# Layer 1 attention: GpSimd's additions of probabilities, each split into two of 512 columns

## The chip, the core and the metric

The kernel runs on one core of a Trainium2 chip. The core has five engines that each work through a program of their own and wait for one another by semaphores: TensorE (PE in the profile, its weight loads PEld), VectorE (DVE), ScalarE (ACT), GpSimd (POOL) and SyncE (SP), which issues the DMAs here. The metric is the device time of one execution in microseconds, from three runs before the change.

## What is computed

Two layers, each an attention and a feed-forward part whose results are multiplied and added to the input x of 4 x 1024 tokens by 512 values. Only layer 1's attention matters here, softmax attention with 16 heads of 32 values:

```python
def proj(w):
    return (x @ w.T).reshape(b, t, NH, HD).transpose(0, 2, 1, 3)
q, k, v = (proj(wq), proj(wk), proj(wv))
q, k = apply_rope(q, k, sin, cos)
att = jnp.einsum('bhqd,bhkd->bhqk', q, k) * (1.0 / math.sqrt(HD))
att = jax.nn.softmax(att, axis=-1)
y = jnp.einsum('bhqk,bhkd->bhqd', att, v)
```

The sum of the exponentials over all keys, by which softmax divides, is what the additions of this change build up.

## The kernel before

Four stages follow one another: layer 0 attention, layer 0 feed-forward, layer 1 attention, layer 1 feed-forward. `layer1_attention` works on 16 groups (4 batches by 4 groups of 4 heads). Its ticks are written out for the first four and the last ones; between them a hardware loop (`Fori` in `ticks`) runs them, two ticks to a pass of its body.

A tick has 32 units. In a unit ScalarE computes the probabilities of one pair of heads for 128 keys and 512 queries: two activations (L1170) read the scores from `ps_sc0` and `ps_sc1` and write the two halves of one of eight tiles `probs` (128x2x512). Units 0 to 15 are for the first 512 queries and 16 to 31 for the rest; inside each, a unit is a block of keys and a pair of heads.

For each unit whose block of keys isn't the first, `add` on GpSimd (L1102) adds the unit's `probs` tile to `summed`, all 1024 columns in one instruction. That is 28 additions a group. In the last group every other one is VectorE's: 434 on GpSimd in all and 14 on VectorE. An addition waits until both activations of its unit are done (`exp_done`) and until the addition two units before is. ScalarE waits, before it writes a tile, for the addition eight units back, since that one reads the same tile (`RING = 8`). At the end of each half TensorE sums `summed` over its partitions (den, L1343), ScalarE copies that (L1145), VectorE inverts it in four pieces (L1253), and GpSimd multiplies the output by it (`y_out`, L1210, 128x512).

In the same tick the next group is prepared, one chunk of 128 tokens in every two units of the first 16, chunks 0 to 7: TensorE projects (L61), ScalarE copies to `qk` and `v` (L1185, L1186), VectorE turns q and k by the rope tables (L1237, L1238, L1239, then L1242), ScalarE casts (L1156, L1158), VectorE subtracts what the cast has kept (L1245 for `q_tok`, L1246 for `k_tok`), TensorE transposes q and k (L1355) into `ps_prep`, and ScalarE copies them to `q_st` and `k_st` (L1198). The six VectorE instructions read both operands from SBUF, as GpSimd's do. Between them VectorE reduces the scores of a first pass from PSUM to their maxima (L1259, one input). TensorE's order in a tick is fixed by `prepare`, `scores`, `pv` and `maximum`; q transposes of a chunk wait for `stacked` (both `q_tok` and `k_tok`) and for the bank `ps_prep` to be read.

Of the kernel before, what the change touches and what calls it, by code (L numbers as in the profile page):

```python
# [7 lines left out]
ALU = mybir.AluOpType  # L8
# [18 lines left out]
def need(eng, sem, count):  # L27

    if isinstance(count, int) and count <= 0:
        return  # L30
    eng.wait_ge(sem, count)  # L31


def live(c, n):

    return not isinstance(c, int) or 0 <= c < n
# [867 lines left out]
def layer1_attention(nc, xt_in, wqkvT, rope_cos, rope_sin, yt_out):  # L904
# [13 lines left out]
    RING = 8  # L918
# [3 lines left out]
    with ExitStack() as ctx:  # L922
# [60 lines left out]
        probs = [sb(f"probs{i}", [P, 2, DIM]) for i in range(RING)]  # L983
# [98 lines left out]
        def adds_with(g, u):  # L1082


            if u < 0:
                g, u = g - 1, u + UNITS
            qb, kt, pair = u // LAST, max(u // 2 % CPB, 1), u % 2
            if isinstance(g, int) and g == NT - 1:
                n = (CPB - 1) * qb + kt
                return (dve_added, n) if pair else (added, ADDS * QB * g + n)  # L1090
            return added, ADDS * (QB * g + qb) + 2 * (kt - 1) + pair + 1

        def add(eng, m, u):

            g, kt, total = m - 1, u // 2 % CPB, summed[u // LAST][u % 2]
            need(eng, exp_done, 2 * (UNITS * g + u + 1))
            if kt > 1:
                need(eng, *adds_with(g, u - 2))
            elif live(g - 1, NT):
                need(eng, prep_done, prep_use(*((m, ("den", 1)) if u >= LAST else (m - 1, ("den", 0))))[1] + 1)  # L1100
            old = probs[(u - 2) % RING] if kt == 1 else total
            eng.tensor_tensor(total[:, :, :], old[:, :, :], probs[u % RING][:, :, :], ALU.add).then_inc(adds_with(g, u)[0], 1)  # L1102

        S = 4
        sched = (0, 4, NT, NT)
# [98 lines left out]
        @block.gpsimd  # L1204
        def _(pool):
            def scale_out(g, qb):
                need(pool, y_copied, QB * g + qb + 1)
                need(pool, y_stored[qb], 16 * g)
                need(pool, inverted, PIECES * (QB * g + qb + 1))
                pool.tensor_tensor(y_out[qb][:, :], y_sb[qb][:, :], inv_den[:, :], ALU.mult).then_inc(y_ready, 1)  # L1210

            def tick(m, p):

                for u in range(UNITS):
                    last = isinstance(m, int) and m == NT
                    if u // 2 % CPB and live(m - 1, NT) and not (last and u % 2):
                        add(pool, m, u)
                    for qb in range(QB):
                        if u == INVERT_AT[qb] + PIECES and live(m - 1 - qb, NT):
                            scale_out(m - 1 - qb, qb)  # L1220
            ticks(pool, *sched, tick)
            scale_out(NT - 1, 1)

        @block.vector
        def _(dve):
# [48 lines left out]
            def tick(m, p):  # L1274
                for u in range(UNITS):
                    if isinstance(m, int) and m == NT and u % 2 == 0 and u and (u - 1) // 2 % CPB:
                        add(dve, m, u - 1)
                    todo = [e[1] for e in maxes(u) if exists(m, e)]

                    for c in range(CPB):  # L1280
                        if u == PREP_STEP * c // 2 + 1 and live(m, NT):
                            for step in range(2):
                                chunk(m, p, c, step)
                                if todo:
                                    maximum(m, todo.pop(0))
                    for a in todo:
                        maximum(m, a)
                    for c in range(CPB):
                        if u == PREP_STEP * c // 2 + 2 and live(m, NT):
                            chunk(m, p, c, 2)  # L1290
                    for qb in range(QB):
                        if 0 <= u - INVERT_AT[qb] < PIECES and live(m - 1 - qb, NT):
                            invert(m - 1 - qb, qb, u - INVERT_AT[qb])
            ticks(dve, *sched, tick)
            add(dve, NT, UNITS - 1)
            for step in range(PIECES):
                invert(NT - 1, 1, step)
# [364 lines left out]
```

## Time and profile before

| | us |
|---|---|
| runs before, median of 3 | 3529.43 |
| lowest and highest run | 3527.44, 3536.01 |
| profiled execution | 3538.25 |
| its span (first to last instruction) | 3536.5 |

The profile is of one execution. Busy shares tell how much an engine works, not who is waited for; that is read from the waits and from the timeline. In the timeline a row is a run of like instructions: start, length, engine, line, operation, what it writes and reads, how many, and in brackets the idle time of its engine before it with what ended that. On VectorE and GpSimd an instruction's length includes what it waits for inside, after its semaphores are satisfied.

### The profile page before, as it was taken

The page shows a single profiled execution, that of the slowest core. Times are in us where ns is not written, and L with a number is a line of the kernel's source. Part 1 is how long each engine was busy: PE and PEld are TensorE (multiplying, and loading weights), DVE is VectorE, ACT ScalarE, POOL GpSimd, SP SyncE. Part 2 cuts the span into 40 slices and gives each one's busy share as a digit, 9 for nine tenths or more (in the row PEclk, how much of TensorE's full clock was granted, in tenths as well). Part 3 has the DMA queues.
Part 4 walks back from the last instruction along what each step waited for, and adds up shares of the span by engine and source line. Part 5 has one row for each costly group of instructions (what it writes and reads, how often), then busy time and mean ns, then how long its engine had stood idle before and what let it go on. Part 6 is the DMA issues. An engine that isn't in the chain of part 4 may idle for free. (4 is left out here: it accounts for less than half of the span.)

```text
span 3536.5 us, 53506 instructions
## 1 busy us (share of the span) xinstructions
PE 3178.8 (90%) x16548; PEld 2231.9 (63%) x16548; DVE 2400.1 (68%) x3422; ACT 1662.3 (47%) x3006; POOL 1501.5 (42%) x1085
## 2 busy tenths in 40 slices
PE   5999999919999996999999989999999939999999
PEld 4766666617888885655555555555555418888887
DVE  4455555478888884788888888888888844444444
ACT  2211121106777774566666666666666622222222
POOL 1000000033333331377777777777777732112111
PEclk9999999959999998899999999999999969999999
DMA  2000000031222223111111111111111032122121
GB/s 83 25 24 24 30 24 24 18 113 66 90 89 89 89 78 127 60 51 54 54 55 55 54 55 50 54 54 49 54 55 54 20 150 75 60 74 68 65 74 48
DMA packets 97104, 215.26 MB, mean 61 GB/s; under 512 B 11408, under 2 KB 27792, under 8 KB 96400
## 3 DMA queue, kind: packets, MB, share of 16 engines
q1 hardware_dynamic: 95472, 210.14, 17.6%
q10 hardware_dynamic: 1440, 2.76, 0.2%
q8 instruction: 95, 1.56, 0.2%
q14 instruction: 97, 0.79, 0.1%
HBM read 162.54 MB, written 50.33 MB: 60 GB/s over the span
## 5 line engine op out<-in xcount | busy, mean ns | idle before, releaser
L1102 POOL TENSOR_TENSOR l_attn_summed<-l_attn_summed,l_attn_probs 128x1024 f32<-128x1024 f32 x372 | 884.8, 2402 | 161.0 <-ACT l_attn_probs L1170 160.7
L1259 DVE TENSOR_REDUCE l_attn_maxima<-l_attn_ps_max 128x2 f32<-128x1024 f32 x512 | 608.9, 1210 | 127.9 <-PE l_attn_ps_max L1367 125.3
L1170 ACT ACTIVATE l_attn_probs<-l_attn_ps_sc 128x512 f32<-128x512 f32 x1024 | 578.7, 601 | 217.7 <-PE l_attn_ps_sc L1323 200.2
L1323 PE MATMUL l_attn_ps_sc<-l_attn_q_st,l_attn_k_st 128*128 128x512 f32 x1024 | 451.9, 454 | 15.4 <-ACT l_attn_probs L1170 12.6
L70 PE MATMUL l_ffn_ps_gu<-l_ffn_w_gu,l_ffn_xt 128*128 128x512 f32 (+1 forms) x1536 | 345.6, 378 | 47.0 <-DMA l_ffn_xt<-xt_chunks 47.0
L1367 PE MATMUL l_attn_ps_max<-l_attn_k_st,l_attn_q_st 96*128 96x512 f32 x1024 | 352.9, 428 | 28.4 <-DVE l_attn_maxima L1259 28.3
L1510 POOL TENSOR_TENSOR l_ffn_mixed<-l_ffn_gate,l_ffn_up 128x512 f32<-128x512 f32 (+1 forms) x96 | 115.2, 1199 | 522.6 <-DVE l_ffn_up L1559 519.0
L70 PEld LDWEIGHTS l_ffn_ps_gu<-l_ffn_w_gu,l_ffn_xt 128*128 128x128 f32 x1536 | 279.7, 189 | 87.6 <-DMA l_ffn_xt<-xt_chunks 48.7
L1323 PEld LDWEIGHTS l_attn_ps_sc<-l_attn_q_st,l_attn_k_st 128*128 128x128 f32 x1024 | 193.9, 194 | 222.0 <-ACT l_attn_probs L1170 139.1
L1308 PE MATMUL l_attn_ps_y<-l_attn_probs,l_attn_v 128*32 128x512 f32 x2048 | 286.1, 632 | 16.5 <-issue 12.3
L61 PE MATMUL l_attn_ps_prep<-l_attn_wqkv_hi,l_attn_xt 128*128 (+1 forms) x1016 | 271.2, 348 | 31.8 <-DMA l_attn_xt<-xt_chunks 30.9
L1367 PEld LDWEIGHTS l_attn_ps_max<-l_attn_k_st,l_attn_q_st 96*128 96x128 f32 x1024 | 193.6, 200 | 120.1 <-DVE l_attn_maxima L1259 76.1
L1102 POOL TENSOR_TENSOR l_attn_summed<-l_attn_probs 128x1024 f32<-128x1024 f32 x62 | 147.6, 2388 | 253.9 <-ACT l_attn_probs L1170 253.8
L281 POOL TENSOR_TENSOR l_attn_rstd<-l_attn_mean_var,l_attn_ln_eps 128x1 f32<-128x1 f32 x32 | 6.1, 190 | 551.0 <-DVE l_attn_mean_var L356 551.0
L70 PE MATMUL l_ffn_ps_fc<-l_ffn_t_fc,l_ffn_ct_hi 128*128 128x512 f32 x512 | 214.8, 420 | 12.8 <-issue 6.6
L61 PEld LDWEIGHTS l_attn_ps_prep<-l_attn_wqkv_hi,l_attn_xt 128*128 128x128 f32 x1016 | 181.3, 191 | 62.2 <-DMA l_attn_xt<-xt_chunks 22.6
L319 ACT ACTIVATE l_attn_ot_hi<-l_attn_ps_o 128x512 fp32r<-128x512 f32 x32 | 19.1, 598 | 400.2 <-PE l_attn_ps_o L494 400.2
L70 PE MATMUL l_ffn_ps_out<-l_ffn_t_proj,l_ffn_ht_hi 128*128 128x512 f32 x512 | 205.4, 401 | 0.0
L70 PE MATMUL l_ffn_ps_fc<-l_ffn_t_fc,l_ffn_ct_lo 128*128 128x512 f32 x512 | 204.6, 400 | 0.0
L70 PE MATMUL l_ffn_ps_out<-l_ffn_t_proj,l_ffn_ht_lo 128*128 128x512 f32 x512 | 202.8, 396 | 0.0
L61 PE MATMUL l_attn_ps_prep<-l_attn_wqkv_lo,l_attn_xt 128*128 (+1 forms) x508 | 173.0, 341 | 0.0
L1245 DVE TENSOR_TENSOR l_attn_q_tok<-l_attn_qk,l_attn_q_tok 128x128 fp32r<-128x128 f32 x128 | 117.8, 921 | 76.0 <-ACT l_attn_k_tok L1158 75.8
(232 smaller groups left out, 6584.7 us busy)
## 6 DMA issues: line engine op xcount, KB each, us to landing
l_attn_xt<-xt_chunks SPq DMA_DIRECT2D x128, 512.0 KB, 3.3
xt_chunks<-l_ffn_xt SPq DMA_DIRECT2D x32, 512.0 KB, 2.8
l_ffn_xt<-xt_chunks SPq DMA_DIRECT2D x32, 512.0 KB, 3.4
l_attn_xin<-in_x SPq DMA_DIRECT2D x32, 256.0 KB, 2.7
s<-l_attn_s_sb SPq DMA_DIRECT2D x32, 256.0 KB, 2.0
l_ffn_xa<-in_x SPq DMA_DIRECT2D x32, 256.0 KB, 2.6
l_ffn_xb<-in_x SPq DMA_DIRECT2D x32, 256.0 KB, 2.9
l_ffn_s_sb<-s SPq DMA_DIRECT2D x32, 256.0 KB, 3.6
```

Source lines behind the costliest of these rows:

```text
L61: mm = pe.matmul(out, a(k), w(k), start=(n == 0), stop=(n == 3 * slices - 1))
L70: mm = pe.matmul(out, a(k), w(k), start=(first and k == ks[0] and n == 0), stop=(last and k == ks[-1] and n == 1))
L281: pool.tensor_tensor(rstd[b][:, :], mean_var[b][:, 1:2], bn_eps[:, :], ALU.add).then_inc(rstd_ready, 1)
L319: act.activation(ot_hi[b][:, :, :], ps_o[:, :, :], ACT.Copy).then_inc(ot_hi_ready, 1)
L1102: eng.tensor_tensor(total[:, :, :], old[:, :, :], probs[u % RING][:, :, :], ALU.add).then_inc(adds_with(g, u)[0], 1)
L1170: act.activation(probs[u % RING][:, i, :], ps_sc[i][:, :, :].rearrange("p a n -> p (a n)"), ACT.Exp, scale=ATT_SCALE).then_inc(exp_done, 1)
L1245: dve.tensor_tensor(qs[:, :, 2 * HD:3 * HD], x[:, 0, :, :], fp32(qs[:, :, 0:HD]), ALU.subtract).then_inc(stacked, 1)
L1259: dve.tensor_reduce(maxima[:, j, h:h + 2, half:half + 1], ps_max[bank][:, :, :], AX.X, ALU.max).then_inc(max_read[bank], 1)
L1308: mm = pe.matmul(ps_y[HD * h:HD * h + HD, :], v[p][:, kt, HD * h:HD * h + HD], probs[(2 * j + h // 2) % RING][:, h % 2, :], start=(kt == 0 ...
L1323: pe.matmul(ps_sc[i][:, :, :].rearrange("p a n -> p (a n)"), k_st[p][:, h, P * kt:P * kt + P], q_st[p][:, h, DIM * qb:DIM * qb + DIM], sta ...
L1367: mm = pe.matmul(dst[:, i, :], q_st[b][0:AUG, h + i, P * j:P * j + P], k_st[b][0:AUG, h + i, DIM * half:DIM * half + DIM], start=True, sto ...
L1510: pool.tensor_tensor(mixed[p][:, lo:hi], gate[p][:, lo:hi], up[p][:, lo:hi], ALU.mult).then_inc(mixed_ready, 1)
```

## The change

`add` issues two instructions, one for each head of the pair (`i` is 0 or 1), each of 128x512. Only the second one counts up the semaphore. The waits ahead of the first are as before, and so is the place of every addition in its engine's order. `add` is also what VectorE runs in the last group, so its 14 additions are split in the same way.

```diff
             old = probs[(u - 2) % RING] if kt == 1 else total
-            eng.tensor_tensor(total[:, :, :], old[:, :, :], probs[u % RING][:, :, :], ALU.add).then_inc(adds_with(g, u)[0], 1)
+            for i in range(2):
+                ins = eng.tensor_tensor(total[:, i, :], old[:, i, :], probs[u % RING][:, i, :], ALU.add)
+            ins.then_inc(adds_with(g, u)[0], 1)
```

## Rows read from the trace of the kernel before

**Rows 1.** The page, section 1: busy us of each engine.

```profile
PE 3178.8 (90%) x16548; PEld 2231.9 (63%) x16548; DVE 2400.1 (68%) x3422; ACT 1662.3 (47%) x3006; POOL 1501.5 (42%) x1085
```

**Rows 2.** Busy time by stretch: stretch, length, then busy us of each engine.

```profile
core 0: us, PE busy (x) PEld busy (x) DVE busy (x) ACT busy (x) POOL busy (x), PEclk, DMA share, GB/s
1451.00:2804.00 1353.00, 1231.12 (x6584) 730.85 (x6584) 1117.05 (x1347) 875.56 (x1857) 1020.65 (x446) 0.97 0.16 52
```

**Rows 3.** Waits of PE, 1451 to 2864: total us, times, longest us.

```profile
PE l_attn_ps_max L1367 <- DVE l_attn_maxima L1259: 25.6, 45, 1.2
PE l_attn_ps_sc L1323 <- ACT l_attn_probs L1170: 12.6, 41, 0.9
...
PE l_attn_ps_prep L1355 <- DVE l_attn_k_tok L1246: 10.5, 34, 0.7
```

**Rows 4.** The page, section 5: busy us, mean ns, then idle before, and its releaser.

```profile
L1102 POOL TENSOR_TENSOR l_attn_summed<-l_attn_summed,l_attn_probs 128x1024 f32<-128x1024 f32 x372 | 884.8, 2402 | 161.0 <-ACT l_attn_probs L1170 160.7
...
L1102 POOL TENSOR_TENSOR l_attn_summed<-l_attn_probs 128x1024 f32<-128x1024 f32 x62 | 147.6, 2388 | 253.9 <-ACT l_attn_probs L1170 253.8
```

**Rows 5.** Groups of instructions of DVE in the stage, same columns.

```profile
L1242 DVE TENSOR_TENSOR l_attn_qk<-l_attn_turned_part,l_attn_swapped 128x128 f32<-128x128 f32 x128 | 154.3, 1205 | 1.8
...
L1245 DVE TENSOR_TENSOR l_attn_q_tok<-l_attn_qk,l_attn_q_tok 128x128 fp32r<-128x128 f32 x128 | 117.8, 921 | 76.0 <-ACT l_attn_k_tok L1158 75.8
L1246 DVE TENSOR_TENSOR l_attn_k_tok<-l_attn_qk,l_attn_k_tok 128x128 fp32r<-128x128 f32 x128 | 101.5, 793 | 0.0
```

**Rows 6.** Timeline of DVE in chunk 0 of one group.

```profile
1815.92 1.38 DVE L1237 TENSOR_TENSOR l_attn_turned_part<-l_attn_qk,l_attn_cos_t 128x128 f32<-128x128 f32 x1 [2.80 <-ACT l_attn_qk L1185]
...
1817.37 0.21 DVE L1239 TENSOR_TENSOR l_attn_swapped<-l_attn_qk,l_attn_sin_t 128x64 f32<-128x64 f32 x1
...
1818.63 0.28 DVE L1242 TENSOR_TENSOR l_attn_qk<-l_attn_turned_part,l_attn_swapped 128x128 f32<-128x128 f32 x1
...
1819.97 1.33 DVE L1245 TENSOR_TENSOR l_attn_q_tok<-l_attn_qk,l_attn_q_tok 128x128 fp32r<-128x128 f32 x1
1821.23 0.28 DVE L1246 TENSOR_TENSOR l_attn_k_tok<-l_attn_qk,l_attn_k_tok 128x128 fp32r<-128x128 f32 x1
```

**Rows 7.** Timeline of POOL, DVE, ACT and PE in chunk 5 of the same group.

```profile
1843.01 4.79 POOL L1102 TENSOR_TENSOR l_attn_summed<-l_attn_summed,l_attn_probs 128x1024 f32<-128x1024 f32 x2 [2.18 <-ACT l_attn_probs L1170]
1845.48 2.47 DVE L1246 TENSOR_TENSOR l_attn_k_tok<-l_attn_qk,l_attn_k_tok 128x128 fp32r<-128x128 f32 x1
1847.26 0.60 ACT L1198 ACTIVATE l_attn_k_st<-l_attn_ps_prep 128x512 fp32r<-128x512 f32 x1 [0.83 <-PE l_attn_ps_prep L1355]
1848.00 0.47 PE L1355 MATMUL l_attn_ps_prep<-l_attn_ident_r,l_attn_q_tok 128*96 128x128 f32 x4 [0.24 <-DVE l_attn_k_tok L1246]
```

**Rows 8.** Timeline of POOL through units 18 to 31 and beyond.

```profile
1783.16 4.71 POOL L1102 TENSOR_TENSOR l_attn_summed<-l_attn_probs 128x1024 f32<-128x1024 f32 x2 [7.07 <-ACT l_attn_probs L1170]
1787.84 18.73 POOL L1102 TENSOR_TENSOR l_attn_summed<-l_attn_summed,l_attn_probs 128x1024 f32<-128x1024 f32 x8
1806.53 1.28 POOL L1210 TENSOR_TENSOR l_attn_y_out<-l_attn_y_sb,l_attn_inv_den 128x512 f32<-128x512 f32 x1
1807.77 9.39 POOL L1102 TENSOR_TENSOR l_attn_summed<-l_attn_summed,l_attn_probs 128x1024 f32<-128x1024 f32 x4
1818.67 2.48 POOL L1102 TENSOR_TENSOR l_attn_summed<-l_attn_probs 128x1024 f32<-128x1024 f32 x1 [1.51 <-ACT l_attn_probs L1170]
```

**Rows 9.** Timeline: ACT's activations of unit 31, PE's q transposes of chunk 0.

```profile
1808.34 1.30 ACT L1170 ACTIVATE l_attn_probs<-l_attn_ps_sc 128x512 f32<-128x512 f32 x2 [0.83 <-PE l_attn_ps_sc L1323]
...
1821.89 0.41 PE L1355 MATMUL l_attn_ps_prep<-l_attn_ident_r,l_attn_q_tok 128*96 128x128 f32 x4
```

**Rows 10.** Timeline of POOL and DVE at the same place, behind the loop's branch.

```profile
2078.05 9.31 POOL L1102 TENSOR_TENSOR l_attn_summed<-l_attn_summed,l_attn_probs 128x1024 f32<-128x1024 f32 x4
...
2088.72 0.29 DVE L1237 TENSOR_TENSOR l_attn_turned_part<-l_attn_qk,l_attn_cos_t 128x128 f32<-128x128 f32 x1 [1.94 <-ACT l_attn_qk L1185]
```

**Rows 11.** Timeline of POOL and PE at the stage's end.

```profile
2861.20 6.72 POOL L1102 TENSOR_TENSOR l_attn_summed<-l_attn_summed,l_attn_probs 128x1024 f32<-128x1024 f32 x2
...
2868.01 1.94 PE L1343 MATMUL l_attn_ps_prep<-l_attn_summed,l_attn_ones 128*32 128x512 f32 x8 [2.56 <-POOL l_attn_summed L1102]
```

## Prediction

> **What bounds the kernel now.** I read the busy shares first: TensorE is busy for 90% of the span, VectorE 68%, GpSimd 42% [rows 1]. The change touches one stage alone, layer 1's attention, so the next view is the stage's own stretch. In 1353 us of it (all but its start and its end) TensorE is busy for 1231.12 us, VectorE for 1117.05 and GpSimd for 1020.65 [rows 2]. TensorE leads and its 122 us of gaps are the most that anything in this stage could give back. The table of waits says who ends them [rows 3]: VectorE's maxima 25.6 us, ScalarE's probabilities 12.6 us, VectorE's k_tok 10.5 us. GpSimd is in none of these rows. Its 434 additions of 128x1024 take 884.8 + 147.6 = 1032.4 us, and 161.0 + 253.9 = 414.9 us of idle time stand before them, nearly all of it until ScalarE has written the probabilities [rows 4]. So GpSimd follows; it doesn't lead.
>
> It does act on VectorE. The instructions with two SBUF operands that make q and k (L1242, L1245, L1246) have means of 1205, 921 and 793 ns [rows 5], and the same instructions take 0.28 us when GpSimd is idle [rows 6]. In the three groups that is 154.3 + 117.8 + 101.5 = 373.6 us against 384 x 0.28 = 107.5 us, so about 266 us of VectorE's time is waiting inside its own instructions. The plainest case is a k_tok of 2.47 us [rows 7]: GpSimd's two additions run from 1843.01 to 1847.80, and k_tok starts at 1845.48, one boundary (about 1845.4) after which the second addition had begun, and ends at 1847.95, 0.15 us after it. I read this as: a two-operand VectorE instruction waits until GpSimd's current instruction ends, gets through at that boundary, and the next one waits for the next boundary. Reductions from PSUM (L1259) do not show it.
>
> **Price of a split addition.** Removed: 434 additions on GpSimd and 14 on VectorE (last group) of 1024 columns. Added: twice as many of 512. GpSimd's eight additions in a row take 18.73 us, 2.34 each from start to start, and a 512-column instruction in the same run (y_out) starts at 1806.53 with the next at 1807.77: 1.24 us [rows 8]. Two are 2.48, so a split addition costs 0.14 us more. The low bound is zero (time by columns alone); the high bound, from y_out's own 1.28 us taken twice against 2.34, is 0.22. I take 0.14, because it is start to start on both sides. In all 434 x 0.14 = 61 us more on GpSimd, against 414.9 us of idle time. That would be free if it were spread evenly. [...]
>
> **Where the 61 us aren't free.** In the second part of each group (units 16 to 31) GpSimd has no idle time. From 1783.16 its 14 additions and one y_out run back to back until 1817.16 [rows 8]. With the change this run ends 14 x 0.14 = 2.0 us later, at about 1819.1. Two things could wait for it. The first is ScalarE, which may not write a probability tile before the addition eight units back has read it. The last two activations of the group start at 1808.34 [rows 9] and the last addition ends at 1817.16: 8 us of lag, some 3.5 additions, out of 8. With 2.0 us more it is about 4.5. This wait stays away.
>
> The second is chunk 0 of the next group, where VectorE starts q and k just as this run ends. In the trace L1237 begins at 1815.92, is held until 1817.30, L1238 and L1239 then pass an idle GpSimd, and L1242 starts at 1818.63, 0.04 us ahead of GpSimd's next addition at 1818.67, and takes 0.28 us. L1245 is held until 1821.30, k_tok ends at 1821.51 [rows 6], and TensorE, which starts the q transposes at 1821.89 [rows 9], has some 0.3 us to spare. With the change the boundaries are 1816.64, 1817.88 and 1819.12: L1237, L1238 and L1239 each wait for one, and the chain leaves at about 1819.25 instead of 1817.58. A maximum of 1.15 us follows, so L1242 starts at about 1820.35. GpSimd's next addition, ready since 1818.67, runs 1819.12 to 1821.60 with a boundary at 1820.36. If L1242 catches that boundary k_tok is done at about 1822.0 and TensorE loses 0.1 to 0.4 us. If it misses, it waits until 1821.6, k_tok ends near 1823.3, and TensorE loses about 1.5 us. I take 0.6 us for such a group.
>
> This holds for about half of the groups. The loop's body has two groups, and after its branch all engines start later: there GpSimd's run ends at 2087.36 and L1237 starts only at 2088.72 [rows 10]. A run that ends at 2089.3 then costs L1237 one boundary (0.6 us), after which GpSimd has nothing to do, and k_tok has spare time. So **+8 x 0.6 = +5 us** for chunk 0.
>
> **The other seven chunks.** Here VectorE's waits get shorter, which is what a split can give. For the k_tok of 2.47 us the halves end at about 1844.25, 1845.5, 1846.75 and 1848.0; q_tok goes at 1845.5, k_tok at 1846.75, about 1.1 us earlier. But TensorE's q transposes at 1848.00 also need the bank that ScalarE's k_st copy frees, and this copy ends at 1847.86 [rows 7], 0.14 us ahead; that copy follows TensorE's transposes of the chunk before, whose k_tok was done long ago. What is late next is thus equally late, and almost nothing comes back, although the row is labelled k_tok. Most of the 10.5 us [rows 3] is of this kind: I take **-1 us**. In chunks 1 and 2 L1242 is released earlier and ScalarE's casts with it, so v's copy may be some 0.1 us earlier: two chunks by 15 groups is -3 us. Against that q_tok and k_tok leave when GpSimd's burst of two additions ends, and a burst ends 0.28 us later, some 0.1 us of which may show: +2 us. Together **-1 us**. VectorE's maxima (25.6 us) mostly hold TensorE in the second part, where VectorE has maxima and reciprocals and nothing with two SBUF operands, so they don't move: 0.
>
> **The end of the stage.** TensorE's last den waits for GpSimd's last addition: the two last additions run 6.72 us from 2861.20, and den starts at 2868.01 after 2.56 us of idle time [rows 11]. They alternate with VectorE's additions, split as well. Two splits are 0.28 us, and handing over at twice as many boundaries about as much again: **+0.5 us**.
>
> **Sum.** +5 - 1 - 1 + 0.5 = +3.5 us, from 3538.25 (span 3536.5 and 1.75 us around it) to about 3542. The profiled execution is 8.8 us above the median of the runs, 3529.43; the same difference on the median gives 3533. What a measurement of this kernel can tell from no change is about 0.3%, 10.6 us, so this is a forecast of no difference.
>
> **Rivals.**
> First, faster: VectorE's shorter waits do reach TensorE. For it: 266 us of waiting is much, and k_tok and maxima together end 36.1 us of TensorE's gaps [rows 3]. Halved, with ScalarE's later copies moving up as well: -18 us, 3511. Against it: the tie of k_tok with k_st, and that a chain of two-operand instructions under a busy GpSimd leaves only where the burst ends. It would need TensorE's order to have no other late input. The Trainium skill's "SBUF — State Buffer", section "Who interferes with whom", says that VectorE with two SBUF inputs and a GpSimd instruction that reads SBUF exclude each other for the whole instruction, the second blocking until the first ends. By that rule the longest wait falls from a whole addition to half of one, and it speaks for this rival; the trace agrees with the mechanism, an instruction of 2.47 us beside additions of 2.34 [rows 7, 8].
> Second, slower: the tail of GpSimd's run costs chunk 0 the missed boundary every time, and the groups behind the branch as well. For it: the 0.04 us by which L1242 now gets ahead. Price: 1.5 us by 15 groups is 22 us, 3552. It decides from the point where the run's end passes L1242's lead: 0.04 us of delay on VectorE is enough there, and 14 x 0.14 is far above it. Against it: a missed boundary costs 1.24 us and no longer 2.4, and behind the branch the run ends 1.4 us ahead of chunk 0 [rows 10].
> Third, it doesn't do what it says: GpSimd goes from one half to the other with no wait between them, and VectorE gets no turn there. Then VectorE's waits stay at 2.4 us, only the 61 us are added, and chunk 0 loses by the late run alone: +5 for chunk 0, nothing back, +0.5 at the end, about +6 us, 3535.
>
> **How the numbers follow.** Forecast (3533, within 0.3%) 0.57; faster rival 0.15; slower rival 0.17; no turn between the halves 0.11. The range reaches to the faster rival's milder half and the slower one's: 3516 to 3548. Faster by over 0.3% (below 3518.8): 0.14. Slower by over 0.3% (above 3540.0): 0.20, which is the slower rival and a part of the third. Within: 0.66.
>
> **What would show it.** In the profile after: GpSimd's additions of 512 columns at about 1.3 us each with starts 1.24 us apart; their sum near 1100 us; no long wait of ScalarE on summed; L1242, L1245 and L1246 never over about 1.4 us, with a sum well below 373.6 us (right), or still up to 2.4 us (third rival). In chunk 0, L1237 to L1239 held one after another, and TensorE's wait on k_tok there. If TensorE's wait rows shrink by more than 10 us, the first rival is right. I am wrong as well if a split addition costs much more than 0.14 us: at about 0.5 us each GpSimd's run would reach the ring's eight units.

## The result and the profile after

The changed kernel takes 3565.91 us (median of 4 runs, 3558.22 to 3568.51), the kernel before, run beside it, 3529.24 us (3527.44 to 3536.01). The ratio is 1.0097, with an interval of 1.0076 to 1.0118: the change costs 37 us. The forecast was 3533, and the range ended at 3548. The profiled execution took 3568.51 us, 30.3 us more than that of before, which lay 9.0 us above its median.

The page after, section 1, busy us of each engine [rows 1]:

```profile
PE 3194.1 (90%) x16548; PEld 2242.7 (63%) x16548; DVE 2359.9 (66%) x3436; ACT 1667.5 (47%) x3006; POOL 1568.9 (44%) x1519
```

GpSimd's additions (before: [rows 4]), then VectorE's instructions for q and k (before: [rows 5]). In the kernel after, every line behind the edit has moved down by two:

```profile
L1103 POOL TENSOR_TENSOR l_attn_summed<-l_attn_summed,l_attn_probs 128x512 f32<-128x512 f32 x744 | 943.5, 1303 | 126.7 <-ACT l_attn_probs L1172 126.4
L1103 POOL TENSOR_TENSOR l_attn_summed<-l_attn_probs 128x512 f32<-128x512 f32 x124 | 157.7, 1297 | 246.7 <-ACT l_attn_probs L1172 246.7
```

```profile
L1244 DVE TENSOR_TENSOR l_attn_qk<-l_attn_turned_part,l_attn_swapped 128x128 f32<-128x128 f32 x128 | 65.8, 514 | 1.8
L1247 DVE TENSOR_TENSOR l_attn_q_tok<-l_attn_qk,l_attn_q_tok 128x128 fp32r<-128x128 f32 x128 | 67.4, 527 | 73.9 <-ACT l_attn_k_tok L1160 73.5
L1248 DVE TENSOR_TENSOR l_attn_k_tok<-l_attn_qk,l_attn_k_tok 128x128 fp32r<-128x128 f32 x128 | 133.6, 1044 | 0.0
```

The additions and these three groups of VectorE behave as forecast. The additions are 943.5 + 157.7 = 1101.2 us (forecast: near 1100), and the three groups of VectorE fell from 373.6 to 266.8 us, with none of their instructions over 1.4 us (before, up to 2.5). L1237, L1238 and L1239, which the prediction's sum left out, grew by 48 us together. The loss is TensorE's. Its waits in the stage, 1451 to 2904 (before: [rows 3]): total us, times, longest us:

```profile
PE l_attn_ps_prep L1357 <- ACT l_attn_q_st L1193: 35.8, 15, 2.4
PE l_attn_ps_max L1369 <- DVE l_attn_maxima L1261: 29.4, 47, 3.9
PE l_attn_ps_prep L61 <- DMA l_attn_xt<-xt_chunks: 23.0, 12, 2.6
...
PE l_attn_ps_prep L1357 <- ACT l_attn_k_st L1200: 9.0, 38, 0.2
PE l_attn_ps_prep L1345 <- DVE l_attn_summed L1103: 4.1, 1, 4.1
```

The largest row, for q_st, was 35.8 us before as well. The row that has grown is the one for xt, and the prediction doesn't mention it. The same row of the kernel before, in 1451 to 2864:

```profile
PE l_attn_ps_prep L61 <- DMA l_attn_xt<-xt_chunks: 7.7, 9, 1.1
```

TensorE now waits 15.3 us longer for a load of `xt`, the input of the next group's projections. The stage as a whole, columns as in [rows 2], before and then after (what comes ahead of 1390 is unchanged, and the last stage takes 660.5 us before, 660.8 after):

```profile
1390.00:2876.00 1486.00, 1334.23 (x7040) 784.93 (x7040) 1200.54 (x1459) 938.59 (x1986) 1072.66 (x466) 0.96 0.16 52
```

```profile
1390.00:2906.00 1516.00, 1350.49 (x7040) 797.37 (x7040) 1159.83 (x1474) 945.12 (x1987) 1138.80 (x900) 0.94 0.16 51
```

The stage is 30 us longer. 13.7 us of that are idle time of TensorE (151.8 to 165.5). The other 16.3 us are busy time for the same 7040 matmuls: the mean granted clock fell from 0.96 to 0.94. Counted in the trace's clock record from the first group to the last, TensorE's clock was at 1.2 GHz for 71.7 us before and for 109.2 us after.

Where in the stage: 3.3 us lie ahead of the first group and of the first addition. In the thirteen traces of this study that point lies anywhere from 1449.8 to 1455.9 us, so this is no effect of the change. From there TensorE's entries into each half of a group (its matmuls on `minus_max`) cut the stage into parts. The first parts (units 0 to 15) of 15 groups have grown by 23.3 us, that of the last group by 4.8, and the second parts are 1.8 us shorter in all. Before, a first part takes about 52 us, and about 54 in four of the five groups behind the loop's branch; after, it takes 53 to 56 in all but the first.

**One place.** Where group 4 is followed by group 5, in the kernel before (SPq is SyncE's queue of DMAs; `y_out` is in [rows 8]):

```profile
1808.25 0.40 SPq L1128 DMA_DIRECT2D yt_chunks<-l_attn_y_out  x1
1809.01 0.94 SPq L1115 DMA_DIRECT2D l_attn_xt<-xt_chunks  x2
1813.00 0.61 PE L61 MATMUL l_attn_ps_prep<-l_attn_wqkv_hi,l_attn_xt 128*128 x2 [0.90 <-DMA l_attn_xt<-xt_chunks]
```

and after:

```profile
1814.57 1.30 POOL L1212 TENSOR_TENSOR l_attn_y_out<-l_attn_y_sb,l_attn_inv_den 128x512 f32<-128x512 f32 x1
1816.31 0.40 SPq L1130 DMA_DIRECT2D yt_chunks<-l_attn_y_out  x1
1817.07 0.94 SPq L1117 DMA_DIRECT2D l_attn_xt<-xt_chunks  x2
1821.08 0.61 PE L61 MATMUL l_attn_ps_prep<-l_attn_wqkv_hi,l_attn_xt 128*128 x2 [2.36 <-DMA l_attn_xt<-xt_chunks]
...
1823.33 0.84 PE L61 MATMUL l_attn_ps_prep<-l_attn_wqkv_hi,l_attn_xt 128*128 x2
1825.05 0.83 DVE L1239 TENSOR_TENSOR l_attn_turned_part<-l_attn_qk,l_attn_cos_t 128x128 f32<-128x128 f32 x1 [5.31 <-ACT l_attn_qk L1187]
```

This is a chain of five links. `y_out` of the first 512 queries stands in GpSimd's queue behind ten additions of the second half. SyncE stores it to DRAM, and in SyncE's queue the loads of `xt` for the next group stand behind that store. The first load is issued 0.76 us after the store and TensorE's projections start 4.0 us after the load, before and after alike. Against the end of unit 31's last activation, `y_out` starts 3.1 us ahead in nearly every group before and 1.7 us ahead in nearly every group after: ten splits at 0.14 us are 1.4 us. TensorE's wait grows by the same, from 0.90 to 2.36 us. And behind this longer gap the granted clock falls to 1.2 GHz: a pair of L61 takes 0.84 us instead of 0.52. In the 10 us from the first L61 on the mean granted clock is 1.00 before and 0.83 after. A pair at 0.84 has lost 0.32 us, 38%; of the 37.5 us more at this clock that makes some 14 by estimate, about the 16.3 us of busy time. Before, the clock fell at the start of 4 groups, all behind the loop's branch, now at that of 14. That the longer gap brings the lower clock is argued from this, and it isn't so every time: in the profile of experiment 1's first kernel, gaps of 1.9, 2.5 and 2.2 us before L61 (at 1543, 1816 and 1909 us) had the full clock for 10 us behind them.

VectorE is hardly held at this place. In the whole trace after, ahead of the last group, a single two-operand instruction was passed over at a boundary of GpSimd's (L1239 at 1551.16, 1.63 us).

**The last group**, in which VectorE makes half of the additions (before, the end was [rows 11]):

```profile
2838.53 5.75 DVE L1103 TENSOR_TENSOR l_attn_summed<-l_attn_probs 128x512 f32<-128x512 f32 x2
2839.55 2.52 POOL L1103 TENSOR_TENSOR l_attn_summed<-l_attn_probs 128x512 f32<-128x512 f32 x2
...
2845.47 0.73 PE L1369 MATMUL l_attn_ps_max<-l_attn_k_st,l_attn_q_st 96*128 96x512 f32 x2 [3.93 <-DVE l_attn_maxima L1261]
...
2890.05 9.01 DVE L1103 TENSOR_TENSOR l_attn_summed<-l_attn_summed,l_attn_probs 128x512 f32<-128x512 f32 x6
2891.77 6.74 POOL L1103 TENSOR_TENSOR l_attn_summed<-l_attn_summed,l_attn_probs 128x512 f32<-128x512 f32 x4
2899.20 1.08 PE L1345 MATMUL l_attn_ps_prep<-l_attn_summed,l_attn_ones 128*32 128x512 f32 x4 [4.14 <-DVE l_attn_summed L1103]
```

Two halves on VectorE take 5.75 us beside GpSimd's run, and a maximum that stands behind them comes 3.9 us late. At the very end the six halves of VectorE and the four of GpSimd alternate. Den waits 4.14 us instead of 2.56, and now for VectorE. From the start of the last group to its middle TensorE takes 34.0 us instead of 29.2.

### The profile page after: what moved, and what is told of

It is laid out like the page before. It is cut to its first block and busy times, and to the rows that moved or that the text cites. A ratio compares the mean times of both kernels' runs of the same rounds, so it can differ in the third digit from the quotient of the medians.

```text
span 3566.8 us, 53954 instructions
## 1 busy us (share of the span) xinstructions
PE 3194.1 (90%) x16548; PEld 2242.7 (63%) x16548; DVE 2359.9 (66%) x3436; ACT 1667.5 (47%) x3006; POOL 1568.9 (44%) x1519
## 5 line engine op out<-in xcount | busy, mean ns | idle before, releaser
L1103 POOL TENSOR_TENSOR l_attn_summed<-l_attn_summed,l_attn_probs 128x512 f32<-128x512 f32 x744 | 943.5, 1303 | 126.7 <-ACT l_attn_probs L1172 126.4
L61 PE MATMUL l_attn_ps_prep<-l_attn_wqkv_hi,l_attn_xt 128*128 (+1 forms) x1016 | 280.8, 359 | 48.4 <-DMA l_attn_xt<-xt_chunks 47.2
L1310 PE MATMUL l_attn_ps_y<-l_attn_probs,l_attn_v 128*32 128x512 f32 x2048 | 287.3, 634 | 15.3 <-issue 11.1
L1103 POOL TENSOR_TENSOR l_attn_summed<-l_attn_probs 128x512 f32<-128x512 f32 x124 | 157.7, 1297 | 246.7 <-ACT l_attn_probs L1172 246.7
L61 PEld LDWEIGHTS l_attn_ps_prep<-l_attn_wqkv_hi,l_attn_xt 128*128 128x128 f32 x1016 | 186.8, 197 | 81.5 <-issue 41.8
L61 PE MATMUL l_attn_ps_prep<-l_attn_wqkv_lo,l_attn_xt 128*128 (+1 forms) x508 | 178.5, 351 | 0.0
L61 PE MATMUL l_attn_ps_proj<-l_attn_wqkv_hi,l_attn_xt_hi 128*128 128x512 f32 x384 | 161.1, 420 | 2.3 <-DVE l_attn_xt_lo L360 1.4
```

Of the source, the lines that this page charges most:

```text
L61: mm = pe.matmul(out, a(k), w(k), start=(n == 0), stop=(n == 3 * slices - 1))
L1103: ins = eng.tensor_tensor(total[:, i, :], old[:, i, :], probs[u % RING][:, i, :], ALU.add)
L1310: mm = pe.matmul(ps_y[HD * h:HD * h + HD, :], v[p][:, kt, HD * h:HD * h + HD], probs[(2 * j + h // 2) % RING][:, h % 2, :], start=(kt == 0 ...
```

## Experiments

Each is compared with the kernel before, run beside it on the same chip (its median was 3532.18 us for experiments 1 and 4, 3532.21 us for 2, 3 and 6). Only the timed ratios carry a verdict; the profile of each is one execution.

**1. Which half of the change.** Split only units 16 to 31 (the diff), or only units 0 to 15 (`u < LAST` in its place), in all groups but the last:

```diff
+            if u >= LAST and not (isinstance(m, int) and m == NT):
+                for i in range(2):
+                    ins = eng.tensor_tensor(total[:, i, :], old[:, i, :], probs[u % RING][:, i, :], ALU.add)
+                ins.then_inc(adds_with(g, u)[0], 1)
+            else:
                 eng.tensor_tensor(total[:, :, :], old[:, :, :], probs[u % RING][:, :, :], ALU.add).then_inc(adds_with(g, u)[0], 1)
```

> Only the additions of units 16 to 31 are split, and none in the last group. Theory A: all of the delay of y_out is made here, so the groups are as slow as in the changed kernel (+2 us in most, about +25), without the 5 us of the last group: 3553 to 3561. Theory B: part of it, as chunk 0 also meets a late run, but first-part additions keep 2.4 us waits: 3545 to 3560.

Measured: 3560.47 us, ratio 1.0083 (1.0064 to 1.0103). Waits of TensorE:

```profile
PE l_attn_ps_prep L61 <- DMA l_attn_xt<-xt_chunks: 24.8, 14, 2.5
PE l_attn_ps_prep L1360 <- DVE l_attn_k_tok L1251: 9.9, 34, 0.9
```

> Only the additions of units 0 to 15 are split, and none in the last group. Theory A: GpSimd has idle time there, y_out isn't later, so nothing is lost: 3526 to 3532. Theory B, or any cost of shorter instructions against VectorE (more boundaries, more waits in a chain): slower by 5 us or more, 3535 to 3550.

Measured: 3527.59 us, ratio 0.9986 (0.9976 to 0.9996). Waits of TensorE:

```profile
PE l_attn_ps_prep L61 <- DMA l_attn_xt<-xt_chunks: 7.3, 9, 1.3
PE l_attn_ps_prep L1360 <- DVE l_attn_k_tok L1251: 0.6, 1, 0.6
```

The loss comes from the second half's additions, where VectorE has nothing to gain. In the first half, where its two-operand instructions are, the split is worth 4.6 us (1.4 to 8.5 by the interval), and TensorE's wait for k_tok goes with it.

**2. The last group alone.** Only the last group's additions are split:

```diff
+            if isinstance(m, int) and m == NT:
+                for i in range(2):
```

> Only the last group's 28 additions are split (14 on GpSimd, 14 on VectorE). The trace of the changed kernel had the stage's end 4 to 5 us longer, with one VectorE half-addition of 4.1 us: +4 to +5 us, 3533 to 3537. If that long wait only came from GpSimd's late run ahead of the last group, +1 us or less.

Measured: 3536.11 us, ratio 1.0010 (1.0000 to 1.0019), so +3.9 us. Its first part is 33.3 us instead of 29.2. The three parts of the change add up to 28.3 - 4.6 + 3.9 = 27.6 us, against 36.7 for the whole; the intervals of the whole and of the first term are 7 us wide to each side, so these can't tell whether the remaining 9 us are real.

**3. No split at all, only a later run.** One spare addition of 128x512 on GpSimd in each group but the last, directly ahead of `y_out`, and in another kernel directly behind it. The run is then 1.24 us longer, but VectorE's boundaries are as before:

```diff
+        spare = sb("spare", [P, DIM])
...
+                            if qb == 0 and not last:
+                                pool.tensor_tensor(spare[:, :].rearrange('p (a n) -> p a n', n=P), fp32(w_hi[:, 0, :, 0:P]), fp32(w_hi[:, 1, :, 0:P]), ALU.add)
```

> The kernel before, no addition split, with one spare addition of 512 columns on GpSimd in each group but the last, right ahead of the y_out of the first 512 queries (its result is used by nobody). It makes y_out and the end of GpSimd's run later by some 1.24 us, the split by 1.4 and 2.0 us. Theory C (the harm is the lateness of that run, by whichever end it reaches TensorE: SyncE's queue behind y_out, or VectorE's two-operand instructions in chunk 0): groups lose as in the changed kernel, some +2 us in most, 3545 to 3557. Theory D (the harm is in the shorter additions themselves): at most the 0.9 us waits grow a little, 3530 to 3535.

Measured ahead of `y_out`: 3557.84 us, ratio 1.0074 (1.0057 to 1.0091). Its wait rows and the timeline at one place:

```profile
PE l_attn_ps_max L1370 <- DVE l_attn_maxima L1262: 28.0, 48, 1.9
PE l_attn_ps_prep L61 <- DMA l_attn_xt<-xt_chunks: 21.7, 12, 2.6
...
PE l_attn_ps_prep L1358 <- DVE l_attn_k_tok L1249: 8.2, 31, 0.8
```

```profile
1810.53 1.28 POOL L1222 TENSOR_TENSOR l_attn_spare<-l_attn_wqkv_hi 128x512 f32<-128x512 f32 x1
1811.77 1.30 POOL L1211 TENSOR_TENSOR l_attn_y_out<-l_attn_y_sb,l_attn_inv_den 128x512 f32<-128x512 f32 x1
1813.01 9.34 POOL L1103 TENSOR_TENSOR l_attn_summed<-l_attn_summed,l_attn_probs 128x1024 f32<-128x1024 f32 x4
1813.51 0.40 SPq L1129 DMA_DIRECT2D yt_chunks<-l_attn_y_out  x1
```

> The same spare addition, but right behind that y_out: y_out, its store and the load of chunk 0 are on time, only the run's end is 1.24 us later. Theory A (all by SyncE's queue): 3530 to 3533. Theory C with both ends: VectorE's L1237 in chunk 0 waits until the later end and TensorE waits for k_tok or maxima: 8 groups by 0.6 to 2 us, 3535 to 3548; the share of the queue is then e5 less this one.

Measured behind `y_out`: 3546.08 us, ratio 1.0038 (1.0027 to 1.0049); its ten runs lie between 3535.5 and 3553.8. Its wait rows, and the timeline:

```profile
PE l_attn_ps_max L1370 <- DVE l_attn_maxima L1262: 32.2, 51, 1.9
PE l_attn_ps_prep L1358 <- DVE l_attn_k_tok L1249: 14.1, 40, 0.9
PE l_attn_ps_prep L61 <- DMA l_attn_xt<-xt_chunks: 9.7, 11, 1.6
```

```profile
1817.06 9.40 POOL L1103 TENSOR_TENSOR l_attn_summed<-l_attn_summed,l_attn_probs 128x1024 f32<-128x1024 f32 x4
...
1824.02 2.58 DVE L1240 TENSOR_TENSOR l_attn_turned_part<-l_attn_qk,l_attn_cos_t 128x128 f32<-128x128 f32 x1 [2.82 <-ACT l_attn_qk L1186]
```

A spare addition ahead of `y_out` brings 25.6 us of loss (just above the 3545 to 3557 expected), most of what the split of the second half cost (28.3 us), with the same wait on xt, first parts of about 54 us as well, and 102.4 us at 1.2 GHz. So a later run is enough for most of the loss, without any halves. VectorE has little part in it: the rows for its maxima and k_tok are 28.0 and 8.2 us here, 25.6 and 10.5 in [rows 3], and none of its instructions is passed over at a boundary.

The same 1.24 us behind `y_out` cost 13.9 us, in another way: VectorE reaches chunk 0 while GpSimd still runs. In the row above it starts 0.1 us ahead of a boundary (about 1824.12), isn't let through there, and ends with the run at 1826.5. This happens in 6 of the 15 groups, and VectorE's maxima and k_tok then hold TensorE for 6.6 + 3.6 us more than in [rows 3].

The difference, 12 us, is what a late `y_out` adds to a late end. It can't be read as SyncE's share of the first loss with 13.9 us as VectorE's, since the two don't add: where the load is late, VectorE doesn't meet the run. A late `y_out` with an end on time was not tried.

**4. The store out of the way.** The store of `y_out` is issued two chunks later, behind the loads of `xt` for chunk 0 and the next ones, once with the change and once with the kernel before:

```diff
+                    if c == 2 and live(m - 2, NT):
+                        store(m - 2, 0)
...
-                if live(m - 1, NT):
-                    store(m - 1, 0)
...
+            store(NT - 1, 0)
```

> The changed kernel, but SyncE issues the store of y_out for the first 512 queries only after the loads of chunks 0 and 1 of the group after, so that no load of xt stands behind GpSimd's y_out. Theory A (GpSimd's run ends later, y_out comes 10 x 0.14 = 1.4 us later, its store holds up SyncE's queue, chunk 0's load lands late, and TensorE waits 2.4 us and then runs at half clock): the waits of PE on xt_chunks vanish, first parts of groups fall from 54.5 to 51 or 52 us where they were 52.0 before, about 25 us back; some 5 us stay at the stage's end: 3530 to 3540. Theory B (chunk 0's two-operand instructions on VectorE, as in the prediction): the queue makes no difference, 3560 to 3566.

Measured: 3571.34 us, ratio 1.0108 (1.0091 to 1.0124), no better than the change itself. The wait on xt is gone. In its place:

```profile
PE l_attn_ps_max L1370 <- DVE l_attn_maxima L1262: 58.9, 63, 3.9
```

```profile
1823.45 6.27 POOL L1103 TENSOR_TENSOR l_attn_summed<-l_attn_summed,l_attn_probs 128x512 f32<-128x512 f32 x5
1825.52 6.80 DVE L1240 TENSOR_TENSOR l_attn_turned_part<-l_attn_qk,l_attn_cos_t 128x128 f32<-128x128 f32 x1 [1.83 <-ACT l_attn_qk L1188]
...
1829.68 2.49 POOL L1103 TENSOR_TENSOR l_attn_summed<-l_attn_probs 128x512 f32<-128x512 f32 x2
...
1833.78 0.74 PE L1370 MATMUL l_attn_ps_max<-l_attn_k_st,l_attn_q_st 96*128 96x512 f32 x2 [2.86 <-DVE l_attn_maxima L1262]
```

Both expectations failed, and this row says why: chunk 0 reaches VectorE earlier and deeper in GpSimd's run, and a turning instruction of 0.28 us takes 6.80. It passes five boundaries of GpSimd without a turn and ends at 1832.32, 0.15 us after the run does. Nine groups have one of 6.7 to 7.1 us. The late load had been sheltering VectorE. So the store's place in SyncE's queue explains the wait on xt, but taking this one path away doesn't give the loss back.

> The kernel before with the same later store and no split. Theory A: the wait of 0.9 us on xt_chunks that some eight groups had before vanishes too, with what TensorE's clock lost after it: 8 x 1 to 1.5 us, 3517 to 3522. Theory B: no difference, 3529.

Measured: 3532.48 us, ratio 0.9999 (0.9988 to 1.0009). The gain that I expected isn't there. The wait on xt (7.7 us) is gone, the one on k_tok has grown by 2.9 us, and in two groups the turning instruction takes 2.7 us or more:

```profile
PE l_attn_ps_prep L1356 <- DVE l_attn_k_tok L1247: 13.4, 36, 0.9
```

**5. How VectorE is served.** The prediction had it that VectorE gets through at every boundary. To measure this away from all else, one small addition of two SBUF operands (`probe`, 128x32 by the rows, not 128x64 as the expectations say; result unused) was put on VectorE in the second half, where it otherwise has none; `(19, 22)` was `(20, 24)` in the second kernel and `(19, 21)` in the third:

```diff
+                    if u == (19, 22)[p] and live(m - 1, NT) and not (isinstance(m, int) and m == NT):
+                        dve.tensor_tensor(probe[:, p, :], cos_t[:, 0:2, :].rearrange('p a n -> p (a n)'), cos_t[:, 2:4, :].rearrange('p a n -> p (a n)'), ALU.add)
```

> The kernel before, with one more small VectorE addition of two SBUF operands (128x64) in the second part of each group but the last: in unit 19 in every other group and in unit 22 in the others. Its result is used by nobody; all else is as before. It measures what VectorE pays for such an instruction by how long GpSimd's run of additions has already gone on. Alone it would take about 0.2 us. Theory (in a long run VectorE gets no turn at the boundaries between GpSimd's instructions): in unit 19, where the run has had one to three additions, at most 2.5 us, let through at the first boundary; in unit 22, where it is six or so deep, several boundaries missed, 5 us or more, and TensorE waits for the maxima behind it. Rival (VectorE gets through at every boundary, as my prediction had it; the long waits come from something at the run's end): at most 2.5 us at both places. Second rival (a back-to-back run starves VectorE from its very start): 5 us and more at both places. Time: within 0.4% of the kernel before unless the waits are over 5 us.

Measured (one run, 3540.01 us beside 3533.68): 2.20 to 2.34 us in unit 19 (7 groups), 0.78 to 0.81 in unit 22 (8 groups). The theory failed at unit 22; by this run alone the first rival holds. One place in unit 22: GpSimd's run has gone on for 8.7 us, as in the other groups (6.3 us if a gap of 0.1 us is taken as its start), and the probe gets through at the next boundary. The activations that the addition behind this boundary needs ended at 1700.61, 1.0 us before it.

```profile
1696.94 9.41 POOL L1103 TENSOR_TENSOR l_attn_summed<-l_attn_summed,l_attn_probs 128x1024 f32<-128x1024 f32 x4
...
1699.39 1.22 ACT L1171 ACTIVATE l_attn_probs<-l_attn_ps_sc 128x512 f32<-128x512 f32 x2
1700.92 0.79 DVE L1293 TENSOR_TENSOR l_attn_probe<-l_attn_cos_t 128x32 f32<-128x32 f32 x1
```

> As the run with the probes in units 19 and 22, with the probes in units 20 and 24 instead. Theory: in unit 20 still mostly one boundary (up to 2.5 us), in unit 24, eight or more additions deep, several boundaries missed, 5 us or more, until the maxima that wait behind it on VectorE hold TensorE and with it ScalarE so long that GpSimd runs out of probabilities. Rival: at most 2.5 us at both. Together the four places give the depth of the run from which VectorE is no longer let through.

Measured (one run, 3602.19 us): 1.23 to 1.31 us in unit 20 (7 groups). In unit 24, 0.27 us in one group and 7.17 to 7.22 us in the seven others, as the theory had it. One of those:

```profile
1704.53 11.65 POOL L1103 TENSOR_TENSOR l_attn_summed<-l_attn_summed,l_attn_probs 128x1024 f32<-128x1024 f32 x5
...
1707.11 0.60 ACT L1171 ACTIVATE l_attn_probs<-l_attn_ps_sc 128x512 f32<-128x512 f32 x1 [0.68 <-PE l_attn_ps_sc L1326]
...
1709.03 7.20 DVE L1293 TENSOR_TENSOR l_attn_probe<-l_attn_cos_t 128x32 f32<-128x32 f32 x1
...
1718.22 1.22 PE L1370 MATMUL l_attn_ps_max<-l_attn_k_st,l_attn_q_st 96*128 96x512 f32 x2 [6.77 <-DVE l_attn_maxima L1260]
...
1719.99 0.60 ACT L1171 ACTIVATE l_attn_probs<-l_attn_ps_sc 128x512 f32<-128x512 f32 x1 [8.89 <-PE l_attn_ps_sc L1326]
```

The probe misses three boundaries. It holds up the maxima, TensorE waits for these, ScalarE gets no scores, GpSimd has no more probabilities to add, and only when its run has ended for that reason does the probe get through (1716.18 and 1716.23). The second parts with such a probe take 44.6 to 47.2 us instead of about 37.4, seven times: some 57 of the 68.5 us.

> The changed kernel (every addition in two halves of 512 columns) with the same extra VectorE addition in units 19 and 21, result unused. It tells whether the starvation goes by time, by the number of instructions of GpSimd's run, or neither. If boundaries let VectorE through early in the run: at most 1.3 us in unit 19. If it goes by the number of instructions, unit 21 of the split kernel (8 or more instructions deep) already shows waits of several boundaries, 4 us or more, while the unsplit kernel in unit 20 or 22 does not. If it goes by time, unit 21 is still at one boundary, 1.3 us. Rival (every boundary lets it through): at most 1.3 us at both.

Measured (one run, 3550.94 us): 1.19 to 1.26 us in unit 19, 0.44 to 0.59 in unit 21, where five halves of the run are over, 7 us from its start: let through each time. In unit 24 of the kernel above five whole additions were over as well, after 13.9 us, and seven of eight weren't let through. So a number of instructions doesn't decide.

What goes with it shows when every such boundary in the traces is counted. I took the two-operand instructions of VectorE in twelve of the thirteen kernels (not the one with the split in the last group alone) ahead of the last group, with the first boundary each meets at which GpSimd goes on with an addition. For that addition I took how long its probabilities had been ready when it started, its lag. For a second half, the lag is that of its first half. Up to a lag of 1.3 us, all 1592 were let through. At 1.5 us it was 1 of 8, all of them the probes of unit 24. From 4.7 us on it was 0 of 31. Between these no case occurred. And one that missed its first boundary missed nearly all that followed too (53 missed, 3 passed at a lag of 0.1 us), even where the lag had fallen to 1.5 us, until GpSimd stood still. GpSimd's lag grows along its run, so lag and time since the run's start can't be told apart by these runs. Both exclude my rule.

**6. What is left of the change.** Split the first half's additions alone, and issue the store late:

> Additions of units 0 to 15 split (none in the last group), and the later store of e4. If the gain of e2 (5 us) and the removed wait on xt_chunks add up: 3518 to 3525. If removing that wait only lets VectorE meet GpSimd's run (as e4 showed with L1237 at 2.8 us), it stays at 3525 to 3530.

Measured: 3518.85 us, ratio 0.9961 (0.9947 to 0.9975), the fastest version. (The first half's split alone, 3527.59 us, is the only other one whose interval lies below the kernel before.) One of its waits:

```profile
PE l_attn_ps_prep L1361 <- DVE l_attn_k_tok L1252: 2.3, 3, 0.9
```

The wait on xt is gone and that on k_tok is 2.3 us. Either edit alone left the other's wait (13.4 us for k_tok, 7.3 for xt). Most first parts without a branch ahead are now 50.7 us instead of 52, and 51.2 us are at 1.2 GHz. The two alone give +0.3 and -4.6 us, together -13.4. That the two late inputs stood in for each other would explain the direction; how the gain divides between waits and clock wasn't tried.

## Why the prediction was wrong

**Price of a split, 0.14 us: right.** 1.24 us from start to start held (ten additions ahead of `y_out` moved it by 1.4 us), and the run's end moved from 7.5 to 9.4 us behind the end of unit 31's last activation; forecast +2.0.

**"Two things could wait for it": the step that failed.** The list of who waits for GpSimd's run had ScalarE's ring of probabilities and VectorE's chunk 0. It left out `y_out`, which stands in the run itself, and behind `y_out` the store in SyncE's queue, and behind the store the loads of `xt`. The evidence was in the trace of before: SPq's rows and TensorE's 7.7 us of waits for `xt`, which said that in nine groups this chain already ended at TensorE, with nothing to spare. [Rows 3] had three of the waits and not this one. (Nor the longest: q_st 35.8 and den 12.1 us, both unchanged after.) By this chain alone 1.4 us a group was to be expected, some 20 us (15.3 came in this wait), and 16.3 us of busy time at the lower clock came with it.

**Chunk 0, +5 us: wrong.** It was worked out along VectorE with a TensorE that arrives on time. In the changed kernel VectorE starts later than GpSimd's run costs it (1825.05, with 5.31 us of idle time before, and L1239 held for 0.83 us). The first parts ahead of the last group lost 23 us in the trace, with one instruction of VectorE passed over. The loss of chunk 0 by VectorE is real, but only where the load is on time: it was 13.9 us with the run's end alone late, and with the store out of the way it took the place of the whole wait on xt (3571 us).

**The boundary rule: right in short runs, wrong in a long one.** It was read from additions that ran two at a time [rows 7] and applied to the tail of 14. Deep in that run VectorE gets no turn (0 of 31 from a lag of 4.7 us on). In [rows 6] L1237 was held until the run ended, which fits both readings. I took the one that the other chunks had shown. The price of "a missed boundary", 1.24 us, was therefore a price for the wrong thing. In the changed kernel itself this error cost little, as the late load came first.

**The other chunks, -1 us: right in kind.** VectorE's waits shrank, TensorE's row on k_tok fell from 10.5 to 0.6 us, and the one on k_st rose from 3.1 to 9.0: the tie that was forecast. The first half alone gave -4.6 us. **The ring** stays away as a cause: five of ScalarE's gaps, 6.5 us in all, bear the label of an addition, each about as long as those at the same units with another label (1.38 or 1.39 us against 1.28 to 1.38, and 0.95 against 0.79 to 0.96).

**The end of the stage, +0.5 us: +4.8 in the trace** for the last group's first part and +1.6 at the very end, where den waits 4.14 us instead of 2.56; +3.9 for both by the experiment. Missed were two halves of VectorE's behind GpSimd's run, 5.75 us, with a maximum behind them.

**The slower rival** had the right sign and 22 of the 37 us, but its mechanism was a boundary missed by L1242. The chain that reached TensorE was another. It deserved more than 0.17, since 2.0 us were added to the end of a chain of which the prediction had shown 0.3 us of slack. **The faster rival** is true of the first half and worth 4.6 us there, not 18. **"No turn between the halves"** is false in short runs.

## What to carry to other kernels

Before a helper engine is made slower, by however little, list everything that stands in its queue behind the work, with each DMA that waits for it and each load that stands behind that DMA on its queue. Idle time elsewhere in the kernel does not pay for a run that has none. Then look whether the chain already ends in a wait of the leading engine: if so, the added time counts nearly in full, and a lower clock may come on top. Then look what stands next behind that wait: here it cost as much once the first was gone. Split where the other engine wants turns, and only there.

## What the runs showed of the hardware

- VectorE instructions with two SBUF operands are let through between two GpSimd instructions as long as GpSimd has hardly fallen behind its inputs (1592 of 1592 up to 1.3 us). When it is some 5 us behind or more, they wait until its run ends: 6.80 us instead of 0.28, past five boundaries. The Trainium skill's "SBUF — State Buffer", section "Who interferes with whom", has the second engine wait until the first one's instruction ends; that agrees with the short runs here, and in the long ones the measured wait is several instructions.
- A delay can shelter another: issuing the load earlier made the changed kernel no faster (3571 us), because VectorE then met GpSimd's run earlier.
- A gap of TensorE of 2.36 us instead of 0.90 was followed by a clock of 1.2 GHz at the start of nearly every group, and in the whole stage by 16 us more of busy time for the same matmuls. Three gaps of 1.9 to 2.5 us in another kernel weren't.
- One extra VectorE instruction in each group made the changed kernel faster in its one run (3551 against 3558 to 3569 us). Where the probe stood in unit 21, `y_out` came 2.4 us ahead of the end of unit 31's last activation instead of 1.7. Why wasn't followed up.
